# Four-layer graph kernel on one core: a bound of three gathers in GpSimd's queue, and the last layer's sum before the gelu on VectorE

## What is computed

```python
s = node_feats @ msg_w[:, :D].T
d = node_feats @ msg_w[:, D:].T
messages = gelu(s[:, None, :] + d[None, :, :] + msg_b)
aggregated = einsum('ijd,ij->id', messages, adj)
combined = concatenate([node_feats, aggregated], axis=-1)
h = gelu(combined @ upd_w.T + upd_b) + node_feats
out = layernorm(h) * ln_w + ln_b     # then: layernorm(node_feats + out)
```

## Time and profile before

| | |
|---|---|
| Median of 3 runs | 946.14 us (941.4 to 949.21) |
| The profiled execution, time | 940.4 us |
| The profiled execution, span from first to last instruction | 938.7 us |
| Busy PE / PEld | 685.3 us (73%) / 402.5 us (43%) |
| Busy DVE / ACT / POOL | 426.3 us (45%) / 365.3 us (39%) / 517.7 us (55%) |
| Mean granted TensorE clock | 0.777 of full speed |
| DMA | 120.80 MB, mean 129 GB/s |

### The profile page before, as it was taken

The page is one execution under the profiler, slowest core; times in us unless marked ns, Lnnn a source line. Parts: engine busy times, 40 slices in busy tenths (PEclk is TensorE's granted clock), DMA queues, the critical chain, the costliest instruction groups (busy, mean ns, idle before and its releaser), DMA issues.

```text
span 938.7 us, 8329 instructions
## 1 busy us (share of the span) xinstructions
PE 685.3 (73%) x2458; PEld 402.5 (43%) x2458; DVE 426.3 (45%) x1529; ACT 365.3 (39%) x591; POOL 517.7 (55%) x513
## 2 busy tenths in 40 slices
PE   1254666999799997989466985285777588589794
PEld 1211142444365644535355633063455356355463
DVE  2298837098986398914435200204413333143222
ACT  0456623468314239654301240134234324442541
POOL 7999199876762067620270067574746656657200
PEclk8669555999879998979655577577979979788685
DMA  8976801799651039930120011111211112111000
GB/s 355 362 283 282 364 1 59 269 409 383 234 186 60 1 133 403 397 150 21 48 60 26 26 40 50 40 50 35 55 32 43 48 37 49 46 45 40 16 6 5
DMA packets 35041, 120.80 MB, mean 129 GB/s; under 512 B 9014, under 2 KB 21748, under 8 KB 25972
## 3 DMA queue, kind: packets, MB, share of 16 engines
q1 hardware_dynamic: 20258, 80.99, 22.3%
q0 software_dynamic: 9888, 38.44, 12.9%
q10 hardware_dynamic: 4846, 0.80, 0.5%
HBM read 114.66 MB, written 5.55 MB: 128 GB/s over the span
## 4 chain that ended last, share of the span: by engine, by line
PE 44%; DVE 12%; another core or an unknown queue 11%; issue 10%; POOL 8%; DMA 8%; ACT 7%; SPq 0%; POOLq 0%; ACTq 0%
PE ps L114 43%; POOL X L924 8%; DMA ring<-in_adjT_dram 8%; ACT dg L1149 2%; DVE Mh L1744 1%; DVE M L1733 1%; ACT L1158 1%; ACT msg L1158 1%; DVE st L1772 1%; DVE w L1617 1%; DVE w L1619 1%; PE ps L1282 1%; DVE Mh L1732 1%; DVE w L1615 1%
## 5 line engine op out<-in xcount | busy, mean ns | idle before, releaser
L913 POOL DMA_INDIRECT G<-near,IX x176 | 176.5, 1003 | 124.2 <-issue 52.4
L924 POOL TENSOR_TENSOR X<-X,ring 128x2708 f32<-128x2708 f32 (+1 forms) x22 | 129.8, 5902 | 25.9 <-DMA ring<-in_adjT_dram 23.1
L114 PE MATMUL ps<-ring,xT_s 128*128 128x512 f32 (+2 forms) x264 | 114.0, 575 | 8.6 <-DMA ring<-in_adjT_dram 8.6
L114 PE MATMUL ps<-ring,hwu 128*128 128x512 f32 (+3 forms) x264 | 117.0, 597 | 1.0 <-ACT hwu L1016 1.0
L1740 DVE COPY listed<-ps 128x386 f32<-128x386 f32 x11 | 6.2, 560 | 238.6 <-issue 85.6
L114 PE MATMUL ps<-G,ident 128*128 128x512 f32 (+1 forms) x88 | 57.9, 743 | 51.3 <-ACT msg L1158 43.5
L1551 DVE FIND_INDEX8 I<-V,rows 128x8 uint32<-128x340 f32 (+2 forms) x176 | 88.1, 504 | 0.0
L1561 DVE MAX8 V<-rows 128x8 f32<-128x340 f32 (+2 forms) x176 | 85.6, 497 | 0.8
L114 PEld LDWEIGHTS ps<-ring,hwu 128*128 128x128 f32 (+1 forms) x264 | 52.0, 207 | 65.9 <-issue 64.6
L114 PE MATMUL ps<-pd,ident 128*128 128x512 f32 (+3 forms) x116 | 70.1, 701 | 6.9 <-issue 4.9
L1023 ACT ACTIVATE binT<-ring 128x2708 bf16<-128x2708 f32 (+1 forms) x22 | 54.0, 2456 | 44.2 <-PE ps L114 36.0
(11 more groups left out here) (245 smaller groups left out, 1109.6 us busy)
## 6 DMA issues: line engine op xcount, KB each, us to landing
ring<-in_adjT_dram SPq DMA_DIRECT2D x48, 1354.0 KB, 12.4
rows<-in_adj_dram POOLq DMA_DIRECT2D x17, 1354.0 KB, 8.8
rows<-in_adj_dram SPq DMA_DIRECT2D x4, 1354.0 KB, 10.5
G<-near,IX POOLq DMA_INDIRECT x176
xT_s<-in_xT_dram SPq DMA_DIRECT2D x1, 1354.0 KB, 6.3
near<-hwu SPq DMA_DIRECT2D x1, 1344.0 KB
out_dram<-yo SPq DMA_DIRECT2D x21, 64.0 KB
near2f<-hwu SPq DMA_DIRECT2D x5, 256.0 KB
```

The lines of the kernel that those rows point to most:

```text
L114: return pe.matmul(dst, lhsT, rhs, start=start, stop=stop, skip_group_check=True)
L913: pool.indirect_dma_start(out=dst, out_offset=None, in_=table, in_offset=bass.IndirectOffsetOnAxis(ap=index, axis=0), bounds_check=N - 1, ...
L924: pool.tensor_tensor(S[0:rn(j), 0:N], S[0:rn(j), 0:N], ring[0:rn(j), j % RING, :], ALU.add).then_inc(o_S, 1)
```

## The change

1. **The bound.** gather counts its calls; from the fourth on GpSimd waits, before each gather, until the third one before it has counted up a new semaphore, o_g, which the gather's engine_sem raises. It holds for the 22 gathers of layer 2 too.
2. **The sum before the gelu.** DVE adds the block's s part, which a matmul with the identity lays in PSUM (own_share), to the eight gathered rows in G3, in place (the new before_gelu), one instruction of 1024 elements a partition. ACT takes one gelu a block, from G3. GpSimd waits for that gelu (c_msg) before it reuses the buffer.
3. **The s part.** Its projection leaves the loop over GROUPS2 and runs behind it, in six chunks without the matmul for the bias; DVE adds the bias, and then d + s for the own messages (own_parts). ScalarE's copies of it and TensorE's matmuls of the own messages go.
4. **Order.** rows_to_list(2) moves behind own_parts; lists(1) goes ahead of the loop over GROUPS2, take_list(1) behind its first step. In the loop over the groups the orders become as the diff shows. The semaphore p_zc is merged into p_sum.

The diff, cut:

```diff
+LEAD = 3
             def gather(dst, table, index, signal):
+                k = next(gathers)
+                if k >= LEAD:
+                    pool.wait_ge(o_g, k - LEAD + 1)
                 pool.indirect_dma_start(out=dst, ...
-                                        bounds_check=N - 1, oob_is_err=False).then_inc(signal, 16)
+                                        bounds_check=N - 1, oob_is_err=False, engine_sem=o_g).then_inc(signal, 16)
...
                     if n >= QUEUE3:
-                        pool.wait_ge(p_pre, 2 * (n - QUEUE3 + 1))
+                        pool.wait_ge(c_msg, n - QUEUE3 + 1)
...
-                if g:
-                    projected3(g - 1)
...
             def messages_own(q):
-                act.wait_ge(p_md, q + 1)
+                act.wait_ge(v_s, 2 * q + 2)
...
             def messages(n):
-                for h in range(2):
-                    act.wait_ge(p_pre, 2 * n + h + 1)
-                    act.activation(msg[0:r, n % 2, 4 * h:4 * h + 4, :], bank((2 * n + h) % 3) ... ACT.Gelu).then_inc(c_msg, 1)
+                act.wait_ge(v_pre, n + 1)
+                act.activation(msg[0:r, n % 2, :, :], G3[0:r, n % QUEUE3, :, :], ACT.Gelu).then_inc(c_msg, 1)
...
             # ScalarE
             for g in range(NG3):
+                if g:
+                    messages_listed(g - 1)
+                    aggregated(g - 1)
                 messages(2 * g)
                 if g:
-                    weights(2 * g + 1)
-                    messages_listed(g - 1)
-                    update(g - 1)
+                    features(g - 1)
+                weights(2 * g + 1)
+                if g:
+                    deviations3(g - 1)
                 messages(2 * g + 1)
                 if 2 * g + 2 < NB:
                     weights(2 * g + 2)
...
             # TensorE
-                for q, n in enumerate(range(first, first + count)):
-                    at = bank(4 + g % 2, q * D, D)[0:rn(n), :]
-                    mm(pe, at, x3T[:, n, 0:rn(n)], w3c[:, D:2 * D], True, False)
-                    last = mm(pe, at, ones[0:1, 0:rn(n)], b3_b[0:1, 0:D], False, True)
-                last.then_inc(p_pr, 1)
+            for q in range(CH):
+                if q >= 2:
+                    pe.wait_ge(v_s, 2 * q - 3)
+                for i, n in enumerate(blocks_of(q)):
+                    last = mm(pe, bank(6 + q % 2, i * D, D)[0:rn(n), :], x3T[:, n, 0:rn(n)], w3c[:, D:2 * D], True, True)
+                last.then_inc(p_pr, 1)
...
+            def own_share(n):
+                if n >= 2:
+                    pe.wait_ge(v_pre, n - 1)
+                mm(pe, bank(n % 2, 0, D)[0:rn(n), :], ident[0:rn(n), 0:rn(n)], pd3[0:rn(n), n, D:2 * D], True, True).then_inc(p_pr, 1)
...
             for g in range(NG3):
-                before_gelu(2 * g)
                 if g:
                     aggregate(2 * g - 1)
                     listed_before_gelu(g - 1)
+                if g + 2 < NG3:
+                    lists(g + 2)
+                if g:
                     aggregate_listed(g - 1)
                     new_features(g - 1)
-                if g + 2 < NG3:
-                    lists(g + 2)
-                before_gelu(2 * g + 1)
+                if 2 * g + 2 < NB:
+                    own_share(2 * g + 2)
                 aggregate(2 * g)
+                if 2 * g + 3 < NB:
+                    own_share(2 * g + 3)
...
             # VectorE
+            def before_gelu(n):
+                r = rn(n)
+                dve.wait_ge(s_g[n % QUEUE3], past2[n % QUEUE3] + 128 * (n // QUEUE3 + 1))
+                dve.wait_ge(p_pr, 2 * CH + n + 1)
+                dve.tensor_tensor(G3[0:r, n % QUEUE3, :, :], G3[0:r, n % QUEUE3, :, :],
+                                  bank(n % 2, 0, D)[0:r, :].unsqueeze(1).broadcast_to([r, TOP, D]), ALU.add).then_inc(v_pre, 1)
+            for q in range(CH):
+                own_parts(q)
+            rows_to_list(2)
+            for g in range(NG3):
+                before_gelu(2 * g)
+                if g:
+                    update(g - 1)
+                if g + 3 < NG3:
+                    rows_to_list(g + 3)
+                before_gelu(2 * g + 1)
+                list_to_rows(g)
+                if g + 2 < NG3:
+                    take_list(g + 2)
+                if g == 1:
+                    checks()
```

More of the change, by code:

```diff
@@ L1 @@
+import itertools
 from contextlib import ExitStack
@@ L961, in _ @@
                     if n >= QUEUE3:
-                        pool.wait_ge(p_pre, 2 * (n - QUEUE3 + 1))
+                        pool.wait_ge(c_msg, n - QUEUE3 + 1)
                     for k in range(TOP):
-                        gather(G3[0:rn(n), n % QUEUE3, k, :], near3[:, :], IX[0:rn(n), n, k:k + 1], s_g[2 * (n % QUEUE3) + k // 4])
+                        gather(G3[0:rn(n), n % QUEUE3, k, :], near3[:, :], IX[0:rn(n), n, k:k + 1], s_g[n % QUEUE3])
                 pool.wait_ge(v_list, g + 1)
@@ L1171, in update, with features @@
                 act.activation(aggS[:, g % 2, 0:P + rn(2 * g + 1)], bank(5, 0, P + rn(2 * g + 1)), ACT.Copy).then_inc(c_aggS, 1)
+            def features(g):
                 act.wait_ge(p_nf, g + 1)
@@ L1193, in _ @@
             messages_listed(NG3 - 1)
-            update(NG3 - 1)
+            aggregated(NG3 - 1)
+            features(NG3 - 1)
+            deviations3(NG3 - 1)
             act.wait_ge(s_out[0], 32 * (NG3 - NG3 // 2))
@@ L1328, in _ @@
                                   selz[0:64, 0:q], True, True)
-                    last.then_inc(p_zc, 1)
+                    last.then_inc(p_sum, 1)
                 if 0 <= s - 1 < CH:
@@ L1760, in _ @@
             for g, (first, count) in enumerate(GROUPS2):
+                normal2(g, first, count)
                 if g == 0:
-                    rows_to_list(2)
-                if g == 1:
                     take_list(1)
-                normal2(g, first, count)
             def normal3(g, signal_at):
@@ L1821, in checks, with own_parts @@
                 dve.tensor_reduce(bads[:, :], bad[:, :], AX.X, ALU.add).then_inc(s_bad, 1)
-            list_to_rows(0)
-            take_list(2)
-            rows_to_list(3)
-            checks()
-            for g in range(1, NG3):
+            def own_parts(q):
+                b = blocks_of(q)
+                dve.wait_ge(p_pr, CH + q + 1)
+                for first, m, r in [(b[0], 4, P)] if q < CH - 1 else [(b[0], 1, P), (b[1], 1, LAST)]:
+                    n = slice(first, first + m)
+                    last = dve.tensor_tensor(pd3[0:r, n, D:2 * D], bank(6 + q % 2, (first - b[0]) * D, m * D)[0:r, :].rearrange(
+                        "p (q w) -> p q w", w=D), b3_b[0:r, 0:D].unsqueeze(1).broadcast_to([r, m, D]), ALU.add)
+                last.then_inc(v_s, 1)
+                dve.wait_ge(v_s, 2 * q + 1)
+                dve.wait_ge(c_d, len(GROUPS2))
+                for first, m, r in [(b[0], 4, P)] if q < CH - 1 else [(b[0], 1, P), (b[1], 1, LAST)]:
+                    n = slice(first, first + m)
+                    last = dve.tensor_tensor(msgd[0:r, n, :], pd3[0:r, n, 0:D], pd3[0:r, n, D:2 * D], ALU.add)
+                last.then_inc(v_s, 1)
+            def before_gelu(n):
[15 more added lines that the diff above has]
+                list_to_rows(g)
                 if g + 2 < NG3:
                     take_list(g + 2)
-                if g + 3 < NG3:
-                    rows_to_list(g + 3)
-                update(g - 1)
-                list_to_rows(g)
+                if g == 1:
+                    checks()
             update(NG3 - 1)
```

63 lines of the change are left out of this document (17 added, 46 removed).

## The result

| | before | after |
|---|---|---|
| Median (20 runs each) | 945.15 us (935.59 to 951.99) | 954.12 us (943.09 to 967.31) |
| Ratio of the times | | 1.0064, 95% interval 1.0033 to 1.0095 |
| Profiled execution: time, span | 940.4, 938.7 us | 943.09, 941.4 us |
| Busy PE, DVE, ACT, POOL | 685.3, 426.3, 365.3, 517.7 us | 584.1, 460.1, 360.5, 517.9 us |
| Mean granted TensorE clock | 0.777 | 0.749 |

The ratio leaves out runs over 1.5% above the fastest of their kernel, so it lies under that of the medians. The forecast was 828 us, with a range from 815 to 895. The kernel is 0.6% slower than the one before. In the kernel after, the gathers are recorded at L920, the gelu of the messages at L1153, the features (hh) at L1171 and DVE's add at L1833.

The account below looks back on a forecast made before the run. The prediction blamed stalls from GpSimd's gather backlog. First gelu done at 541.9, groups of 26.5 us and shorter last ones to 795.3, plus 12.3 and 12.4 of tail and 7.4 to the median, gave 828 us, range 815 to 895.

Parts of the forecast that it names:

- The bound of three: On GpSimd: at most three gathers queued should end the 35 us stall of the other engines and the later ones.
- The 35 us freeze: Last layer, about 571 to 606 us: other engines stall during 46 unbroken gathers, read as semaphores delayed by GpSimd's queued gathers.
- the rival that named it: Last layer: limiting queued gathers does not lift the stalls, only the earlier start is left, 919 us; chance 0.16.
- The stretch from 700 to 770: Profile window of the kernel before, taken as one without a stall: PE busy 53.16 of 70 us.
- The cost of the bound: GpSimd's gathers: the added wait and increment cost nothing, each gather keeps 1.303 us.
- The rival with 63 us: GpSimd's gathers: the wait costs 0.30 us at each of 209 gathers, 885 us in all; chance 0.11.
- The earlier start: End of layer 2: without the s projection in each step, last-layer gathers start at 516.7 us, 26.7 us earlier.
- DVE's add: Each block of the last layer: VectorE's sum of 1024 elements before the gelu takes 1.2 us.
- The 24 us kept for hindered gathers: Last-layer gathers: 22 adds on VectorE might each slow one gather by 1.1 us; counted only in the range.
- The ring: Last layer's group loop: dependencies from one gelu through TensorE, ScalarE and VectorE to the next set 26.5 us a group.
- The sum: Whole kernel: start, ten groups and tail give a span of 820.0, plus 7.4 to the median, 828 us.
- The rival for the other side: Last layer: stalls stay and each of ten groups has one of 8.3 us, 961 us, slower; chance 0.03.

Follow-up runs that it names:

- e5: The kernel after, unchanged, in a job with freezes: 939.72 us, ratio 1.0013 to the kernel before.
- e6: The kernel after without the wait that limits queued gathers to three, in a job with freezes: 942.41 us, ratio 1.0018 to the kernel before.
- e2: The kernel before with only the limit of three queued gathers added, in a job without freezes: 861.96 us, ratio 0.9993.
- e11: The kernel after, unchanged, in a job without freezes: 830.66 us, ratio 0.9661 to the kernel before.

## Why the prediction was wrong

- **The bound of three: the step that failed.** "The 35 us freeze and the later ones go, if the backlog is their cause." It isn't: 48.1 us with the bound, 48.30 without (e5, e6). This step held most of the forecast gain, and the rival that named it had 0.16. The timing it rested on is seen again (engines come free 5.2 us after GpSimd's run ends), but it fits a cause in the running gathers as well as one in the queued ones; the rows couldn't separate them. "The 22 gathers of layer 2 froze nobody" holds for the trace of before, but after the change two waits of 3.63 and 6.51 us stand there. The stretch from 700 to 770, which stood for one without a freeze, holds the wait of 8.34 us at 746.31.
- **The cost of the bound: right.** Gathers start 1.30 us apart with the wait, and e2 is at 0.9993. The rival with 63 us falls.
- **The earlier start: right.** Forecast 26.7 us, without freezes 540.86 - 511.95 = 28.9. From the second on, full steps of 6.12 us between d copies, forecast 6.05. In the profile after it is 19.8 us; the two waits in layer 2, 10.1 us together, cover the missing 9.1.
- **DVE's add: right.** 1.22 us (forecast 1.2), the gelu of 1024 1.06. The 24 us kept for hindered gathers did not come: the gathers' mean was 1.017 us in e11 against 1.008 in e2, 1.6 us over 176. So the Trainium skill ("SBUF — State Buffer", Who interferes with whom), by whose rule this term is 0, and the trace agree closely.
- **The ring: right in size, one term missed.** Forecast 26.5 us a group, measured 27.0 (604.19 to 739.27, five groups, e11). From hh to the end of the gelu it is 14.2 us instead of 12.7: ACT's table load of 1.28 us comes only when DVE's add is done, and the sum has no term for it. The other half, with the clock, was forecast at 13.8 and took 13.0.
- **The sum.** It gives 827.4, rounded to 828, for a measured 830.66 without freezes. Errors of opposite sign cancel in part: the start came 2.2 us earlier than forecast, and the table load was missed. That is luck. But what I subtracted from was wrong in kind: there the old order needs 862, and the loop is no shorter after (301.9 against 300.3 us). The whole gain is the earlier start.
- **The rival for the other side** had 0.03: freezes stay, and DVE in the ring adds one to each group, 961 us. The record is 954.12. Its mechanism is the one seen: in seven groups aggS, and in five hh, wait 5 to 13 us. It was priced as five more of 8.3 us, 41.5; measured are 30.1 us more of freezes in all. That the longer ring is the reason, with its hand-overs between TensorE, ScalarE and VectorE, and not the gathers' earlier place, was not tested.

What stays open: what holds the hand-overs back while gathers run (semaphores, the engines' instruction streams or the recording), why some jobs have it and others not, and whether spacing prevents it. That the gathers are needed for it rests on when it comes: in no profile does an unnamed wait stand ahead of the first gather of layer 2, and in e5 the last gather starts at 865.17, and the groups behind it take 22.57 and 27.06 us, as without freezes:

```profile
866.59 0.38 ACT L1171 ACTIVATE hh<-ps 128x256 f32<-128x256 f32 x1 [5.77 <-remote]
889.16 0.38 ACT L1171 ACTIVATE hh<-ps 128x256 f32<-128x256 f32 x1 [1.32 <-PE ps L116]
916.22 0.38 ACT L1171 ACTIVATE hh<-ps 128x256 f32<-128x256 f32 x1 [3.55 <-PE ps L116]
```

## What to carry to other kernels

A stall without a named releaser whose cause is only inferred should not carry the largest term of a forecast; price the change once with the stall and once without, and give both a real chance. Where the same kernel has two levels of time in different jobs, compare versions in each of them: here a change worth 3.4% in one is worth nothing in the other. In a long run of gathers beside a ring of short hand-overs, one pause a group may be worth its price in a job with freezes (900 us against 935 for the kernel before and 940 for the one after in another such job; one run) and is a loss in one without (846 to 851 against 831). Before a pause is called one after each block, count the gathers between two pauses in the trace.

## What the hardware showed that I had not expected

- In some jobs an idle ScalarE learns of a matmul up to 44 us after its modelled end while GpSimd issues indirect DMAs of 128 rows, one every 1.30 us; in others, with the same kernel and the same spacing, never. The kernel before takes 935 to 945 us in the one kind and 860 to 863 in the other.
- While the others stand, GpSimd's own wait on o_g is served in time: its gathers keep their 0.30 us of idle. A wait for TensorE at the end of a run can be unnamed on GpSimd too (5.71 us at 608.88 in the earlier trace rows).
- The same chip number had both kinds of job, eleven minutes apart.
- With the freezes, over half of the record's DMA updates of semaphores are missing from the first gather on (1,500 in the profile after, 4,141 in e11).
